# Activation table sets loaded by number, inverse roots from logarithm and exponential, and an expert layer read from a block-diagonal Gelu

## The chip, the cores and the metric

The kernel runs as one launch on one core of a Trainium2 chip. The metric is the device time of that core in microseconds. The core's engines are TensorE (PE in the profile, its weight loads PEld), VectorE (DVE), ScalarE (ACT), GpSimd (POOL) and SyncE (SP); each takes its instructions in order, and they wait for each other through semaphores.

## The reference

The input x is (8, 32, 16, 16): batch 8, 32 channels, 16 by 16 pixels. In float32, cut to what matters:

```python
x = x + conv_attention(_gn(x), ...)   # deformable attention, 4 heads, 16 sampled keys a head:
    # q, offset convolution, off / sqrt(var(off) + 1e-5), gelu, tanh, sigmoid,
    # grid_sample, softmax over 16 keys with a sampled position bias, output projection
t = _to_tokens(x)                     # (8, 256, 32)
t = t + self_attention(_ln_t(t))      # softmax(n @ n.T) @ n
t = t + experts(_ln_t(t), ...)
x = _from_tokens(t, x)

def _ln_t(v, eps=1e-05):
    m = jnp.mean(v, axis=-1, keepdims=True)
    s = jnp.var(v, axis=-1, keepdims=True)
    return (v - m) / jnp.sqrt(s + eps)

# experts: 16 experts, each picks the top 8 of the 256 tokens of a batch
probs = softmax(x @ gate_w.T + gate_b, axis=1)
topv, topi = top_k(probs, 8)                     # per batch and expert
pooled = sum_k topv * x[topi]                    # (8, 16, 32)
h = gelu(einsum('ebd,edh->ebh', [pooled, 1], weight1))   # 128 hidden
out = einsum('ebh,eho->ebo', [h, 1], weight2)            # 32 outputs
outputs[topi] += topv * out
```

Each of the 16 experts has its own `weight2` (128 by 32 and a bias row) and meets 8 rows, one per batch.

## The kernel before

There is no loop over tiles: everything stays in SBUF and PSUM, and the 128 partitions hold (batch, channels of a group), tokens, or (expert, batch) by turns. The order on each engine is written out by hand, with semaphores between the engines. The work runs in this order: group norm and q; convolution offsets with their norm, Gelu and tanh; sampled values and the position bias; attention logits, softmax (`d_max`, `d_sub`, `d_exp`, `d_sum`, `d_rec`, `d_prob`), transposes of the probabilities (L788), copies to `prob_t` (L584) and the attention output (L798); first layer norm (L591 to L596 on ACT, L1051 to L1056 on DVE); self-attention (L807 to L834, exponentials at L604); second layer norm (L619, L623 on ACT, L1076 to L1083 on DVE); gate (L883 to L901); experts (L915 to L933); two stores.

Both norms of tokens work alike, in two halves `h`: ACT squares into `ln_sq` or `u_sq`, DVE sums to `ln_ss`, ACT takes `Sqrt` into `ln_std`, DVE takes the reciprocal into `ln_rstd` and multiplies, giving `t1` or `t2`. PE turns both halves (L807, L876).

ACT needs the table set of a function loaded before it. `load_table(func)` (L503 to L508) runs a one-element activation of `func` on `warm`; the build puts an ACT_TABLE_LOAD ahead of it. It is called eight times: Sqrt, Gelu, Exp, Sqrt (after `d_exp`, L578), Exp (after the first norm's roots), Sqrt (after the copies `ot`, L615), Exp (after the second norm's roots), Gelu (after `g_exp`, L630).

The experts' second layer (L919 to L926) puts the 16 experts in four groups `q` of four. One matmul per group multiplies the 32 columns (expert, batch) of `hidden` with the 128 columns (expert, output) of `w2_sb`, and lands on 32 of the 128 partitions of `out2_ps`. So each row meets four experts' weights, and DVE keeps its own: it multiplies by the mask `row_slot` (L1116), sums over the four (L1117), and then scales for each batch (L1120).

`keep_busy(wait, bank)` (L649 to L652) issues `BUSY[wait]` matmuls of zeros on PE ahead of a wait; nobody reads them.

## Time and profile before

| | us |
|---|---|
| median of 3 runs | 65.18 (64.65, 65.18, 76.61) |
| the profiled execution's own time | 64.59 |
| its span, first to last instruction | 62.8 |

| engine | busy us | share of the span | instructions |
|---|---|---|---|
| PE | 53.7 | 86% | 579 |
| DVE | 38.4 | 61% | 96 |
| ACT | 34.3 | 55% | 70 |
| POOL | 21.0 | 34% | 44 |

The time outside the span is 64.59 - 62.8 = 1.8 us. The busy time of PE holds 16.1 us of zero matmuls (L652, 213 of them), so its share says little about what bounds the kernel. The chain of work that ended last is put down to PE for 46%, ACT 17%, DVE 16%, POOL 7%, and it passes from engine to engine every few tenths of a microsecond. The granted TensorE clock is 1.00 throughout.

### The profile page before, as it was taken

How to read it: one execution, taken by the hardware profiler on the slowest of the kernel's cores; microseconds unless marked ns; L12 is line 12 of the kernel's file. 1: busy time of each engine (PE TensorE's matmuls, PEld its weight loads, DVE VectorE, ACT ScalarE, POOL GpSimd, SP SyncE). 2: the span in 40 equal slices, each digit the busy share in tenths (PEclk: the TensorE clock that was granted, in tenths of full speed). 3: DMA queues.
4: the chain of work that ended last, by engine and by line, in shares of the span. 5: the costliest groups of instructions: out<-in, count | busy, mean ns of one | idle time of the engine just before them, and what ended most of it. 6: DMA issues, size and time to landing. Idle time of an engine off the chain costs nothing.

```text
span 62.8 us, 1442 instructions
## 1 busy us (share of the span) xinstructions
PE 53.7 (86%) x579; PEld 44.1 (70%) x579; DVE 38.4 (61%) x96; ACT 34.3 (55%) x70; POOL 21.0 (34%) x44
## 2 busy tenths in 40 slices
PE   3998997996996999999989939599997898989830
PEld 3997885954785899998979837334485586877700
DVE  3286698918499994599900652789969427540620
ACT  0901053969999041049957794988597628401020
POOL 3030489875779899000600000003000790000000
PEclk9999999999999999999999999999999999999999
DMA  0699921100000000000000000000000000000004
GB/s 0 202 188 229 276 70 47 57 8 0 0 0 0 0 10 0 0 0 0 0 0 0 16 5 0 0 0 0 0 0 0 0 10 0 0 0 0 0 18 149
DMA packets 3926, 2.02 MB, mean 32 GB/s; under 512 B 2640, under 2 KB 3792, under 8 KB 3920
## 3 DMA queue, kind: packets, MB, share of 16 engines
q1 hardware_dynamic: 1424, 1.37, 7.7%
q10 hardware_dynamic: 2496, 0.57, 4.2%
q8 instruction: 4, 0.07, 0.4%
q14 instruction: 2, 0.02, 0.1%
HBM read 1.67 MB, written 0.26 MB: 31 GB/s over the span
## 4 chain that ended last, share of the span: by engine, by line
PE 46%; ACT 17%; DVE 16%; POOL 7%; issue 5%; DMA 4%; DVEq 0%; ACTq 0%
PE ps L733 4%; DMA x_sb<-x_rows 4%; ACT L508 4%; ACT e_tok L604 4%; PE ps L829 3%; PE ps L777 3%; PE ps L726 3%; PE ps L798 3%; PE ps L755 3%; DVE taps L973 2%; POOL w_smp L468 2%; PE ps L813 2%; PE ps L652 2%; DVE off L975 2%; PE ps L933 2%
## 5 line engine op out<-in xcount | busy, mean ns | idle before, releaser
L652 PE MATMUL ps<-zeros 128*128 128x128 bf16 x213 | 16.1, 236 | 1.0 <-DVE zeros L950 1.0
L652 PEld LDWEIGHTS ps<-zeros 128*128 128x128 bf16 x213 | 14.7, 107 | 1.8 <-DVE zeros L950 1.0
L508 ACT ACT_TABLE_LOAD x8 | 10.3, 1283 | 1.8 <-PEq L1163 1.7
L604 ACT ACTIVATE e_tok<-ps,cst 128x1024 f32<-128x1024 f32 (+1 forms) x5 | 4.4, 941 | 1.1 <-PE ps L822 0.9
L381 POOL TENSOR_TENSOR c_scaled<-ln_c,e_sum 128x256 f32<-128x256 f32 x1 | 0.6, 622 | 11.7 <-DVE e_sum L1066 11.7
L1066 DVE TENSOR_REDUCE e_sum<-e_tok 128x4 f32<-128x1024 f32 x3 | 3.6, 1216 | 0.4 <-ACT e_tok L604 0.3
L1004 DVE COPY_PREDICATED ps<-over,ps 128x608 f32<-128x608 uint32 (+1 forms) x4 | 3.1, 778 | 0.8 <-PE ps L705 0.7
L829 PE MATMUL ps<-e_tok,t 128*32 128x256 f32 x32 | 3.1, 385 | 0.2 <-ACT e_tok L604 0.2
L705 PE MATMUL ps<-rpe_blk,minus_hat_rel 128*32 128x168 f32 x64 | 2.8, 316 | 0.5 <-DVE minus_hat_rel L1000 0.5
L491 POOL TENSOR_TENSOR o_n<-ln_c,e_rec 128x256 f32<-128x256 f32 x2 | 1.2, 621 | 5.9 <-DVE e_rec L1084 5.9
L568 ACT ACTIVATE kv<-ps,cst 128x256 f32<-128x256 f32 x4 | 1.7, 470 | 2.7 <-PE ps L726 2.7
L1051 DVE TENSOR_REDUCE ln_ss<-ln_sq 128x8 f32<-128x264 f32 x2 | 0.9, 428 | 3.7 <-ACT ln_sq L591 3.7
L421 POOL TENSOR_TENSOR wblk<-wts,cst 128x256 f32<-128x256 f32 x3 | 2.1, 684 | 2.9 <-DMA wts<-weights 2.9
L705 PEld LDWEIGHTS ps<-rpe_blk,minus_hat_rel 128*32 128x32 f32 x64 | 2.0, 142 | 1.3 <-issue 0.9
L813 PE MATMUL ps<-t_t 32*128 32x256 f32 x24 | 2.3, 400 | 0.8 <-ACT e_tok L604 0.8
L829 PEld LDWEIGHTS ps<-e_tok,t 128*32 128x32 f32 x32 | 1.2, 109 | 2.0 <-ACT e_tok L604 1.4
L376 POOL TENSOR_TENSOR d_prob<-d_exp,d_rec 128x512 f32<-128x512 f32 x1 | 1.1, 1057 | 4.5 <-DVE d_rec L1040 4.5
L574 ACT ACTIVATE d_exp<-d_sub 128x512 f32<-128x512 f32 x1 | 0.6, 629 | 3.4 <-DVE d_sub L1034 3.4
L1033 DVE TENSOR_REDUCE d_max<-ps 128x32 f32<-128x512 f32 x2 | 1.4, 691 | 1.7 <-PE ps L733 1.6
L524 ACT ACTIVATE xn_tok<-ps 128x512 f32<-128x512 f32 x1 | 0.6, 597 | 3.2 <-PE ps L669 3.2
L726 PE MATMUL ps<-xs,wblk 128*128 128x128 f32 x16 | 2.2, 281 | 0.1
L813 PEld LDWEIGHTS ps<-t_t 32*128 32x128 f32 x24 | 1.4, 184 | 1.2 <-ACT e_tok L604 1.2
(183 smaller groups left out, 127.3 us busy)
## 6 DMA issues: line engine op xcount, KB each, us to landing
w_sb<-weight ACTq DMA_DIRECT2D x1, 256.0 KB, 6.4
w_sb<-weight SPq DMA_DIRECT2D x1, 256.0 KB, 5.4
x_nat<-x_rows SPq DMA_DIRECT2D x8, 32.0 KB
wts<-weights SPq DMA_DIRECT2D x1, 192.5 KB, 4.6
cst<-shape_consts SPq DMA_DIRECT2D x1, 192.0 KB, 4.0
x_sb<-x_rows SPq DMA_DIRECT2D x1, 128.0 KB, 2.6
x_sb<-x_rows ACTq DMA_DIRECT2D x1, 128.0 KB, 2.8
cst<-shape_consts SPq DMA_DIRECT2D x1, 128.0 KB, 5.3
```

The source lines that it names most:

```text
L421: return nc.gpsimd.tensor_tensor(dst, src.unsqueeze(2).to_broadcast([P, n_groups, B, width]), same_b.unsqueeze(1).unsqueeze(3).to_broadcas ...
L508: nc.scalar.activation(warm[:, n:n + 1], zeros[:, 0:1], func)
L604: return nc.scalar.activation(dst, scores, ACT.Exp, bias=const("bound"))
L652: mm(bank(n_bank, P), zeros[:, :], zeros[:, :], start=True, stop=True)
L705: last = mm(row_ps[g][nx_rows(nx), 8 * yq:8 * yq + 8, 0:WIN], minus_hat_rel[:, yq, g * P + nx:(g + 1) * P:NK], rpe_blk[:, g].rearrange("p ...
L726: last = mm(kv_ps[w][:, g], wblk[:, 1 + w, gi, g].rearrange("p b o -> p (b o)"), xs[:, gi], start=(gi == 0), stop=(gi == G - 1))
L733: last = mm(lg_ps[:, h, g, :, hh], part[:, g, hh, 8 * h:8 * h + 8].rearrange("p y x -> p (y x)"), back_to_n[:, :].rearrange("p (t j) -> p ...
L755: mm(lg_ps[:, h, g].rearrange("p t k j -> p (t k j)"), q_sb[:, g, h * P:(h + 1) * P], kv[:, 0, g].rearrange("p t k j -> p (t k j)"), start ...
L813: last = mm(bank(s_banks[n][k])[:, M * h:M * h + M], t1_t[C * ((2 * n + k) % B4):C * ((2 * n + k) % B4) + C, n // 2, h * P:(h + 1) * P], t ...
L829: return mm(ot_ps[b // B4][rows], t1[:, h, b], e_tok[:, b, h], start=(h == 0), stop=(h == NHALF - 1))
L1004: return nc.vector.copy_predicated(row_ps[g][:, :, 0:width], mask.bitcast(U32).unsqueeze(2).to_broadcast([P, IMG * HG, width]), row_ps[g][ ...
L1066: reduce(e_sum[:, 2 * n:2 * n + 2], e_tok[:, 2 * n:2 * n + 2], AX.X, ALU.add).then_inc(e_sum_ready, 1)
```

## The change

- The four Sqrt and the four reciprocals of the two token norms become `Ln` and `Exp` with scale -0.5, both on ACT (`inverse_root`), with a wait of ACT for its own `Ln` between them. `ln_std` goes, `ln_log` comes.
- Gelu writes its 128 columns into the diagonal blocks of `hidden_blk` (four groups, four experts by four experts by eight batches), which GpSimd has zeroed at the start. The second layer is one matmul for each expert, 16 in all, with 32 stationary columns of which 8 are not zero, 32 moving ones, and accumulation over the four experts of a group. `out2_ps` has 32 columns, the bias matmul too. The mask and the sum on DVE go; the two scalings read `out2_ps` itself.
- `BUSY` has 0 in place of 12 zero matmuls before the transposes of the probabilities, and 6 in place of 15 before the last matmuls.

```diff
-    "d_prob_ready": 12, "prob_copied": 3, "t1_ready": 20, "t1_copied": 7, "t2_ready": 12,
-    "chosen_ready": 14, "pooled_ready": 4, "hidden_ready": 3, "out2_ready": 15,
+    "d_prob_ready": 0, "prob_copied": 3, "t1_ready": 20, "t1_copied": 7, "t2_ready": 12,
+    "chosen_ready": 14, "pooled_ready": 4, "hidden_ready": 3, "out2_ready": 6,
...
+SQRT_SET, LN_EXP_SET, GELU_SET = 3, 6, 10
...
-        hidden = sb("hidden", [P, NE, B])
-        own = sb("own", [P, E4, C])
-        out2 = sb("out2", [P, C])
+        hidden_blk = sb("hidden_blk", [P, EQ, E4, E4, B])
...
-        out2_ps = bank(7, E4 * C).rearrange("p (e o) -> p e o", e=E4)
+        out2_ps = bank(7, C)
...
+        def hidden_diagonal():
+
+            first = hidden_blk[:, :, 0, 0, :]
+            return bass.AP(tensor=first.tensor, offset=first.offset,
+                           ap=[list(first.ap[0]), [E4 * E4 * B, EQ], [E4 * B + B, E4], [1, B]])
...
+            nc.gpsimd.memset(hidden_blk[:, :, :, :, :], 0.0).then_inc(hidden_zeroed, 1)
...
-            warmed = [0]
-
-            def load_table(func):
-
-                n = warmed[0]
-                warmed[0] += 1
-                nc.scalar.activation(warm[:, n:n + 1], zeros[:, 0:1], func)
-
-            act.wait_ge(zeros_set, 1)
-            load_table(ACT.Sqrt)
+
+            def load_table(functions):
+
+                nc.scalar.add_instruction(mybir.InstLoadActFuncSet(
+                    name=nc.get_next_instruction_name(), act_func_set_id=functions, ins=[], outs=[]))
+
+            load_table(SQRT_SET)
...
-            load_table(ACT.Gelu)
+            load_table(GELU_SET)
...
-            load_table(ACT.Exp)
+            load_table(LN_EXP_SET)
...
-            load_table(ACT.Sqrt)
...
-            for h in range(NHALF):
-                act.wait_ge(ln_ss_ready, h + 1)
-                nc.scalar.activation(ln_std[:, 0, h], ln_ss[:, 0, h], ACT.Sqrt).then_inc(ln_std_ready, 1)
-            load_table(ACT.Exp)
+            def inverse_root(k, h):
+
+                act.wait_ge(ln_ss_ready, NHALF * k + h + 1)
+                nc.scalar.activation(ln_log[:, k, h], ln_ss[:, k, h], ACT.Ln).then_inc(ln_log_ready, 1)
+                act.wait_ge(ln_log_ready, NHALF * k + h + 1)
+                nc.scalar.activation(ln_rstd[:, k, h], ln_log[:, k, h], ACT.Exp, scale=-0.5).then_inc(ln_rstd_ready, 1)
+
+            for h in range(NHALF):
+                inverse_root(0, h)
...
-            load_table(ACT.Sqrt)
...
-                act.wait_ge(ln_ss_ready, NHALF + h + 1)
-                nc.scalar.activation(ln_std[:, 1, h], ln_ss[:, 1, h], ACT.Sqrt).then_inc(ln_std_ready, 1)
-            load_table(ACT.Exp)
+                inverse_root(1, h)
...
-            load_table(ACT.Gelu)
+            load_table(GELU_SET)
+            act.wait_ge(hidden_zeroed, 1)
             act.wait_ge(hidden_done, 1)
-            nc.scalar.activation(hidden[:, :, :], hid_ps.rearrange("p q e b -> p (q e) b"),
-                                 ACT.Gelu).then_inc(hidden_ready, 1)
+            nc.scalar.activation(hidden_diagonal(), hid_ps, ACT.Gelu).then_inc(hidden_ready, 1)
...
-            mm(out2_ps, ident, weight("bias2").unsqueeze(1).to_broadcast([P, E4, C]), start=True, stop=False,
-               skip_group_check=True)
+            mm(out2_ps, ident, weight("bias2"), start=True, stop=False, skip_group_check=True)
             pe.wait_ge(w2_loaded, 16)
             keep_busy("hidden_ready", 4)
             pe.wait_ge(hidden_ready, 1)
-            for q in range(EQ):
-                experts = slice(E4 * q, E4 * q + E4)
-                last = mm(out2_ps[E4 * B * q:E4 * B * q + E4 * B], hidden[:, experts].rearrange("p e b -> p (e b)"),
-                          w2_sb[:, experts], start=False, stop=True, skip_group_check=True)
+            for e in range(E4):
+                for q in range(EQ):
+                    last = mm(out2_ps[E4 * B * q:E4 * B * q + E4 * B],
+                              hidden_blk[:, q, e].rearrange("p f b -> p (f b)"), w2_sb[:, E4 * q + e],
+                              start=False, stop=(e == E4 - 1), skip_group_check=True)
...
-                dve.wait_ge(ln_std_ready, h + 1)
+                dve.wait_ge(ln_rstd_ready, h + 1)
                 dve.wait_ge(ln_c_ready, h + 1)
-                link(nc.vector.reciprocal(ln_rstd[:, 0, h], ln_std[:, 0, h]))
...
-                dve.wait_ge(ln_std_ready, NHALF + h + 1)
-                link(nc.vector.reciprocal(ln_rstd[:, 1, h], ln_std[:, 1, h]))
+                dve.wait_ge(ln_rstd_ready, NHALF + h + 1)
...
-            link(tt(own[:, :, :], out2_ps, const("row_slot").unsqueeze(2).to_broadcast([P, E4, C]), ALU.mult))
-            link(reduce(out2[:, :], own[:, :, :].rearrange("p e o -> p o e"), AX.X, ALU.add))
             for t in range(NT):
                 batches = slice(B4 * t, B4 * t + B4)
-                tt(out2_blk[:, batches], out2[:, :].unsqueeze(1).to_broadcast([P, B4, C]),
+                tt(out2_blk[:, batches], out2_ps.unsqueeze(1).to_broadcast([P, B4, C]),
```

**ScalarE, from the copies `ot` to the copy of the gate's logits** (second layer norm; `u_sq` are the squares, `t_t` the transposed tokens). Before:

```order
L615 ACTIVATE ot<-ps 128x256 [waits ot_done] x2
L508 ACT_TABLE_LOAD
L508 ACTIVATE warm<-zeros 128x1
L619 ACTIVATE u_sq<-ln_c 128x8x32 [waits ln_c_ready] x2
L623 ACTIVATE ln_std<-ln_ss 128x8 [waits ln_ss_ready] x2
L508 ACT_TABLE_LOAD
L508 ACTIVATE warm<-zeros 128x1
L626 ACTIVATE t_t<-ps 128x256 [waits t2_turned]
L628 ACTIVATE logits<-ps 128x256 [waits g_done]
```

Now:

```order
L621 ACTIVATE ot<-ps 128x256 [waits ot_done] x2
L624 ACTIVATE u_sq<-ln_c 128x8x32 [waits ln_c_ready] x2
L598 ACTIVATE ln_log<-ln_ss 128x8 [waits ln_ss_ready]
L600 ACTIVATE ln_rstd<-ln_log 128x8 [waits ln_log_ready]
L598 ACTIVATE ln_log<-ln_ss 128x8 [waits ln_ss_ready]
L600 ACTIVATE ln_rstd<-ln_log 128x8 [waits ln_log_ready]
L629 ACTIVATE t_t<-ps 128x256 [waits t2_turned]
L631 ACTIVATE logits<-ps 128x256 [waits g_done]
```

Two loads and their one-element activations are gone from this stretch, and the two square roots have become four short activations in a row.

**TensorE, from the projected values to the attention output** (`vo` in two products, then transposes of `d_prob`). Before:

```order
L777 MATMUL ps<-woblk_c,kv 128x128 [waits wkvo_ready,v_ready]
L777 MATMUL ps<-woblk_c,kv 128x128 x3
L777 MATMUL ps<-woblk,kv 128x128 x4
L652 MATMUL ps<-zeros 128x128 x12
L788 MATMUL ps<-cst,d_prob 128x128 [waits d_prob_ready0]
L788 MATMUL ps<-cst,d_prob 128x128 x3
L788 MATMUL ps<-cst,d_prob 128x128 [waits d_prob_ready1]
L788 MATMUL ps<-cst,d_prob 128x128 x3
L652 MATMUL ps<-zeros 128x128 x3
L798 MATMUL ps<-vo_c,prob_t 128x128 [waits prob_copied,vo_copied]
```

Now:

```order
L780 MATMUL ps<-woblk_c,kv 128x128 [waits wkvo_ready,v_ready]
L780 MATMUL ps<-woblk_c,kv 128x128 x3
L780 MATMUL ps<-woblk,kv 128x128 x4
L791 MATMUL ps<-cst,d_prob 128x128 [waits d_prob_ready0]
L791 MATMUL ps<-cst,d_prob 128x128 x3
L791 MATMUL ps<-cst,d_prob 128x128 [waits d_prob_ready1]
L791 MATMUL ps<-cst,d_prob 128x128 x3
L655 MATMUL ps<-zeros 128x128 x3
L801 MATMUL ps<-vo_c,prob_t 128x128 [waits prob_copied,vo_copied]
```

The transposes follow straight behind the projections; the 12 zero matmuls between them are gone.

**TensorE, from the experts' first layer to the last matmuls.** Before:

```order
L915 MATMUL ps<-pooled,w_sb 128x32 [waits pooled_ready]
L915 MATMUL ps<-pooled,w_sb 128x32 x3
L919 MATMUL ps<-wts,cst 128x128
L652 MATMUL ps<-zeros 128x128 [waits w2_loaded]
L652 MATMUL ps<-zeros 128x128 x2
L926 MATMUL ps<-w_sb,hidden 32x128 [waits hidden_ready]
L926 MATMUL ps<-w_sb,hidden 32x128 x3
L652 MATMUL ps<-zeros 128x128 x15
L933 MATMUL ps<-chosen,out_blk 128x256 [waits out2_ready] x2
```

Now:

```order
L918 MATMUL ps<-pooled,w_sb 128x32 [waits pooled_ready]
L918 MATMUL ps<-pooled,w_sb 128x32 x3
L922 MATMUL ps<-wts,cst 128x32
L655 MATMUL ps<-zeros 128x128 [waits w2_loaded]
L655 MATMUL ps<-zeros 128x128 x2
L928 MATMUL ps<-w_sb,hidden_blk 32x32 [waits hidden_ready]
L928 MATMUL ps<-w_sb,hidden_blk 32x32 x15
L655 MATMUL ps<-zeros 128x128 x6
L936 MATMUL ps<-chosen,out_blk 128x256 [waits out2_ready] x2
```

Four matmuls of 128 moving columns have become 16 of 32, the bias matmul has 32 columns, and 6 zero matmuls stand where 15 stood.

## Rows read from the trace of the kernel before

**Rows 1.** Instructions of line 508: durations in ns (min/median/max), first and last start, us.

```profile
L508 ACT ACT_TABLE_LOAD  x8: 1283/1283/1283, 1.7 to 52.6; - x8
L508 ACT ACTIVATE warm<-zeros x8: 202/203/203, 2.9 to 53.9; 128x1 f32<-128x1 bf16 x8
```

**Rows 2.** Timeline (start us, us, instruction, idle before and releaser), first Gelu.

```profile
11.02 1.73 PE L652 MATMUL ps<-zeros 128*128 128x128 bf16 x28
...
12.42 0.40 ACT L532 ACTIVATE off_blk<-off_nblk 128x256 f32<-128x256 f32 x1
```

**Rows 3.** Timeline, attention probabilities and their transposes.

```profile
29.73 1.06 POOL L376 TENSOR_TENSOR d_prob<-d_exp,d_rec 128x512 f32<-128x512 f32 x1 [4.47 <-DVE d_rec L1040]
...
30.65 0.69 DVE L376 TENSOR_TENSOR d_prob<-d_exp,d_rec 128x512 f32<-128x512 f32 x1
...
30.93 0.58 ACT L581 ACTIVATE vo_c<-ps 128x512 f32<-128x512 f32 x1
...
30.93 0.83 PE L652 MATMUL ps<-zeros 128*128 128x128 bf16 x12
...
31.60 1.04 PE L788 MATMUL ps<-cst,d_prob 128*128 128x128 f32 x8
...
32.24 1.09 ACT L584 ACTIVATE prob_t<-ps 128x512 f32<-128x512 f32 x2 [0.74 <-PE ps L788]
```

**Rows 4.** Timeline, roots of the first layer norm.

```profile
35.59 0.55 ACT L596 ACTIVATE ln_std<-ln_ss 128x8 f32<-128x8 f32 x2
...
36.41 0.19 DVE L1055 RECIPROCAL ln_rstd<-ln_std 128x8 f32<-128x8 f32 x1
...
36.64 0.42 DVE L1056 TENSOR_TENSOR t<-ln_c,ln_rstd 128x256 f32<-128x256 f32 x1
```

**Rows 5.** Timeline, roots of the second layer norm.

```profile
45.55 0.76 DVE L1076 TENSOR_TENSOR ln_c<-ps,c_scaled 128x256 f32<-128x256 f32 x2
...
46.44 0.71 ACT L619 ACTIVATE u_sq<-ln_c 128x256 f32<-128x256 f32 x2
...
46.87 0.76 DVE L1079 TENSOR_REDUCE ln_ss<-u_sq 128x8 f32<-128x264 f32 x2 [0.57 <-ACT u_sq L619]
...
47.33 0.54 ACT L623 ACTIVATE ln_std<-ln_ss 128x8 f32<-128x8 f32 x2 [0.19 <-DVE ln_ss L1079]
...
48.38 0.42 DVE L1083 TENSOR_TENSOR t<-ln_c,ln_rstd 128x256 f32<-128x256 f32 x1
```

**Rows 6.** Timeline, copy of the second norm's transpose and the gate.

```profile
49.30 0.36 ACT L626 ACTIVATE t_t<-ps 128x256 f32<-128x256 f32 x1
...
49.80 1.10 PE L883 MATMUL ps<-t_t,gate_blk 128*128 128x256 f32 x4
```

**Rows 7.** Timeline, second layer of the experts.

```profile
57.14 0.28 ACT L634 ACTIVATE hidden<-ps 128x128 f32<-128x128 f32 x1 [3.01 <-PE ps L915]
...
57.50 0.43 PE L926 MATMUL ps<-w_sb,hidden 128*32 128x128 f32 x8
...
58.00 0.29 DVE L1116 TENSOR_TENSOR own<-ps,cst 128x128 f32<-128x128 f32 x1 [2.03 <-PE ps L926]
...
58.73 0.49 DVE L1120 TENSOR_TENSOR out_blk<-out,row_rec 128x128 f32<-128x128 f32 x2
```

**Rows 8.** Timeline, other matmuls with 32 stationary columns.

```profile
13.93 0.42 PE L694 MATMUL ps<-wts,off_blk 128*32 128x1 f32 x16
...
53.82 1.19 PE L901 MATMUL ps<-picked_t,t 128*32 128x16 f32 x32
```

**Rows 9.** Line 901 (durations in ns, min/median/max; first and last start, us).

```profile
L901 PE MATMUL ps<-picked_t,t x32: 191/197/199, 53.8 to 54.8; 128*32 128x16 f32 x32
```

**Rows 10.** Timeline, GpSimd at the start.

```profile
0.84 0.23 POOL L417 MEMSET pooled<- 128x128 f32 x1
...
3.98 0.62 POOL L421 TENSOR_TENSOR wblk<-wts,cst 128x256 f32<-128x256 f32 x1 [2.91 <-DMA wts<-weights]
```

**Rows 11.** Stretches: busy us (count) PE, PEld, DVE, ACT, POOL; PEclk, DMA, GB/s.

```profile
57.00:62.80 5.80, 3.00 (x33) 2.06 (x32) 1.58 (x5) 0.66 (x2) 0.00 (x0) 1.00 0.13 45
```

More of the change, by code:

```diff
@@ L185, in build @@
         off_blk = sb("off_blk", [P, G, B, N])
-        warm = sb("warm", [P, 8])
         zeros = sb("zeros", [P, P], BF16)
@@ L237, in build @@
         ln_ss = sb("ln_ss", [P, 2, NHALF, B])
-        ln_std = sb("ln_std", [P, 2, NHALF, B])
+        ln_log = sb("ln_log", [P, 2, NHALF, B])
         ln_rstd = sb("ln_rstd", [P, 2, NHALF, B])
@@ L319, in build @@
         rpe_blk_ready, qpad_zeroed = sem("rpe_blk_ready"), sem("qpad_zeroed")
-        pooled_zeroed, zeros_set = sem("pooled_zeroed"), sem("zeros_set")
+        pooled_zeroed, hidden_zeroed, zeros_set = sem("pooled_zeroed"), sem("hidden_zeroed"), sem("zeros_set")
         q_done, q_copied = sem("q_done"), sem("q_copied")
@@ L343, in build @@
         prob_turned, prob_copied, att_done = sem("prob_turned"), sem("prob_copied"), sem("att_done")
-        ln_c_ready, ln_sq_ready, ln_ss_ready, ln_std_ready = (
-            sem("ln_c_ready"), sem("ln_sq_ready"), sem("ln_ss_ready"), sem("ln_std_ready"))
+        ln_c_ready, ln_sq_ready, ln_ss_ready, ln_log_ready, ln_rstd_ready = (
+            sem("ln_c_ready"), sem("ln_sq_ready"), sem("ln_ss_ready"), sem("ln_log_ready"), sem("ln_rstd_ready"))
         t1_ready, t1_turned = sem("t1_ready"), sem("t1_turned")
```

## The prediction

> **What bounds it now.** I read the chain of waits first, then the timeline around each edited line, then single lines for durations. No engine bounds the kernel. The chain goes from engine to engine, so an edit counts only by what it takes from that chain, and each one below is read where it stands. The eight table loads last 1.283 us each and the one-element activation behind each adds about 0.10 (0.20 long, with the next activation starting 0.11 after it) [rows 1]. That is 10.3 us of loads, four of which go. Most of it is no gain: a load costs only what it keeps the next activation from doing.
>
> **Start.** The set number spares the wait for the zeros and one short activation, at a time when ACT waits for data anyway: nothing.
>
> **First Gelu.** The load stays, the short activation goes. Gelu then starts at 12.31 instead of 12.42 and ends at 12.71. The zero matmuls on TensorE last until 12.75 [rows 2], so they are just no cover. Everything behind moves by 0.10 (between 0 and 0.11: nothing if the zero matmuls turn out the later ones). The load ahead of Exp has the same saving. It brings the copy `win` forward, but TensorE has no gap at the parts made from it, so I count nothing there.
>
> **Softmax to attention output.** The load behind `d_exp` ends ahead of the copy `vo_c` at 30.93, and this copy ends at 31.51, while `prob_t` starts at 32.24, released by the transposes of L788 [rows 3]. So that load was covered, and dropping it gains nothing by itself. The 12 zero matmuls were on the path: the first transpose starts 0.67 behind them (30.93 to 31.60) [rows 3]. What is late next is `d_prob`. GpSimd ends its half at 30.79. TensorE followed the end of another engine's result by 0.08 in the experts (57.42 to 57.50) [rows 7]; with 0.1 to 0.2 for GpSimd's the transposes start at 30.9 to 31.0, against 31.60. DVE ends the other half at 31.34 and four transposes take until about 31.4, so it does not hold them up. Gain 0.62, between 0.5 and 0.67.
>
> **Roots of the first norm.** A root of 8 columns lasts 0.21, by the 0.20 of one column [rows 1]; so ACT's first runs 35.59 to 35.80 and the second, which waits for its sum, 35.93 to 36.14 [rows 4]. Before, the first half then takes a reciprocal of 0.19 on DVE; now it takes an exponential of about 0.21 on ACT: no change, and `t1` of half 0 starts at about 36.07 still (0.34 ahead of the reciprocal behind it). For half 1 the reciprocal stood behind `t1` of half 0 on DVE until 36.41, and `t1` started at 36.64 [rows 4]. Now Ln of half 1 runs 35.93 to 36.14, Exp 36.17 to 36.38, and `t1` follows at 36.41. Gain 0.23. Ends: 0 (if ACT's wait for itself costs 0.1 each time) and 0.25. The load behind the roots goes too. The scores that come next wait for seven zero matmuls and for DVE's copy as well, so I take 0.03 for it, between 0 and 0.1.
>
> **Roots of the second norm.** Here a load was on the path. `u_sq` of half 0 started at 46.44, behind load and short activation, while its input, the first of two sums on DVE, was there at 45.97 (45.55 plus 0.42, the length of the like-sized `t2` row) [rows 5]. Now it starts at 45.99 and half 1, whose input ends at 46.31, at 46.33. Half 1 ends at 46.73 instead of 47.15. The sums `ln_ss` (0.42 each) end at 46.83 and 47.18 instead of 47.63. Ln and Exp: half 0 46.87 to 47.31, half 1 47.21 to 47.65. `t2` of half 1, which must also follow half 0 (47.33) by 0.34, starts at 47.67 instead of 48.38 [rows 5]. Gain 0.71, of which 0.45 is the load and the rest the reciprocals. Ends 0.5 and 0.75. What is late next: `ln_c` on DVE, which waits for the turned-back output.
>
> **Copy before the gate.** `t_t` started at 49.30, in the shadow of a load and its short activation, and the gate's matmuls started 0.14 behind the copy's end, at 49.80 [rows 6]. Only the last 0.11 of that shadow is sure to be the load's: DVE copies the other half at the same time, and TensorE's bias matmul stands ahead of the gate. Gain 0.08, ends 0 and 0.11.
>
> **Second layer.** The Gelu ends at 57.42 and L926 starts at 57.50, with the bias matmul and three zero ones done in time [rows 7]; a shorter bias matmul gains nothing. The four old matmuls (eight passes in the trace) take until 57.97, and the scaling starts at 58.73: 0.76 for mask and sum, which go [rows 7]. Against it stand 16 matmuls, 32 passes, in place of eight. The trace has two bounds for the distance between such passes. At L694 eight matmuls of 32 stationary columns go round the four groups of output partitions, as the new ones will: 16 passes in 0.42. At L901 sixteen stay in one group: 32 passes in 1.19 [rows 8]. One pass of the latter lasts 0.197 by itself [rows 9]. So the passes start (0.42 - 0.20)/15 = 15 ns apart in the one and (1.19 - 0.20)/31 = 32 ns in the other; the old L926, with 128 moving columns over four groups, gives about (0.43 - 0.28)/7 = 21. The new ones rotate like L694, and I take 17 ns: 31 x 0.017 + 0.23 = 0.76, done at 58.26. The scaling starts at 58.28 instead of 58.73, and is no slower from PSUM (the mask took 0.29 from there, the scaling 0.29). Gain 0.45. With 32 ns it is 1.22 and no gain (-0.03); with 15, 0.51. Six zero matmuls at 0.06 (12 took 0.67) [rows 3] end before the first scaling, so cutting them from 15 only keeps them out of the way. The Trainium skill ("TensorE: Matmul & The Clock Gate", section "Wait — 56ns, not 53.3ns?") says that start-to-start never drops below about 25 ns however few columns there are. By it this term would be 31 x 0.025 + 0.23 = 1.0 and the gain 0.2. L694 contradicts it with 15 ns, at one moving column.
>
> **Zeroing.** GpSimd's `pooled` of 128 columns took 0.23, so 512 take at most 0.92; they fit in the 2.91 us that GpSimd waits for the weights [rows 10]. Nothing.
>
> **Sum.** 0.10 + 0.62 + 0.23 + 0.03 + 0.71 + 0.08 + 0.45 = 2.22. Against the profiled execution's own 64.59 this gives 62.4; nothing outside the span changes. That execution agrees with the lowest of the three runs (64.65) and is 0.9% below their median (65.18), so the figure may come out some tenths higher. With all low ends the sum is 1.0 (63.6), with all high ones 2.4 (62.2).
>
> **Rivals.**
> - *The small matmuls are paced by themselves.* For: nothing in the trace has 32 of them in rotation with 32 moving columns, and L901 shows 32 ns. Against: L694. At 32 ns the sum is 1.74 and the time 62.9. If each matmul took 62 ns a pass, 1.92 + 0.23 = 2.15 would make this part 0.94 slower than before, the sum 0.83 and the time 63.8; both L694 and L901 speak against it. The same page of the Trainium skill, same section, has such a figure (about 62 ns a matmul where its sequencer decodes it). Chance 0.15 for the 32 ns, 0.04 for 63.8.
> - *The roots don't overlap.* ACT waits for its own Ln four times, and what is queued behind is the other half. If each wait costs 0.1 to 0.15 more, the norms give 0.5 instead of 0.94: 62.9 at full pace elsewhere, 63.3 together with a slow second layer. For: no row shows a chain of dependent short activations. Chance 0.10.
> - *The loads come back (slower).* If something places a load ahead of each Ln and each Exp as separate functions, eight loads of 1.28 stand in the two chains of roots. All but about 0.5 us of them is on the path, which gives 62.4 + 9.8 = 72. It decides from the second load on a chain: 2 x 1.28 is more than the whole gain. Against it: the program as built holds four loads and no other, and before it held the eight that the trace shows. The Trainium skill ("ScalarE: Activation LUTs", "Table sets: the hidden batching unit") says that a pass of the compiler's back end puts a load before every activation that needs one, and also that one set has both functions. Chance 0.03.
> - *TensorE's clock falls (slower).* 21 zero matmuls go. Before, the granted clock is 1.00, and it is so even in the last stretch, where TensorE is busy for 3.0 of 5.8 us [rows 11]. The gaps in which they stood get shorter, too. At 1.2 GHz from the transposes to the scores, about 3.5 us of TensorE on the path would double: 66. Chance 0.02.
>
> **Numbers.** Chance of the forecast as summed, 62.4 with 61.9 to 62.8 around it: 0.66. Range 61.9 to 63.6: it takes in the slow second layer, the slow roots and most low ends together, and the few tenths between the runs before. This kernel can be told from no change at about 2%, 1.3 us. The sum is below this only with nearly all low ends together, or with matmuls at 62 ns, or where the runs differ: same 0.11. Slower 0.05, from the last two rivals. Faster 0.84.
>
> **What would show it.** Four loads in ACT's row. L791 starting right behind L780, and `prob_t` about 0.7 earlier than before. `u_sq` starting behind `ln_c`, not behind ACT. Each Exp of a root 0.02 to 0.04 behind its Ln. 32 passes of L928 in 0.75 and the scaling 0.03 behind. Wrong would be: passes over 30 ns apart, `t2` held by the zero matmuls ahead of the transposes, a clock below 1.00, or a fifth load.

## The result and the profile after

| | before | after |
|---|---|---|
| median, us | 64.92 (4 runs, 64.62 to 76.61) | 62.70 (4 runs, 62.67 to 62.78) |
| ratio to before, without the 76.61 | | 0.969, 95% interval 0.965 to 0.973 |
| profiled execution, us | 64.59 | 62.78 |
| its span, us | 62.8 | 60.7 |
| what lies outside the span, us | 1.8 | 2.1 |
| zero matmuls | 213 | 192 |

One run of the kernel before took 76.61 us and stays out of the ratio; the other three took 64.62, 64.65 and 65.18. The kernel is 3.1% faster, 62.7 us against a forecast of 62.4 and a range of 61.9 to 63.6. The granted clock stayed at 1.00 in the profile. Below, the lines of after that answer to the rows of before; times are us from the span's start.

The shares by engine of the chain that ended last (part 4 of the page), and the table loads (part 5):

```profile
PE 57%; DVE 11%; ACT 10%; POOL 7%; issue 5%; DMA 4%; DVEq 0%; ACTq 0%
...
L510 ACT ACT_TABLE_LOAD x4 | 5.1, 1283 | 1.7 <-PEq L1162 1.7
```

PE's share rose from 46% to 57% and ACT's fell from 17% to 10%: loads and roots have left the chain. The rise of PE is in part a matter of ties. Zero matmuls hold 6% of this chain (L655, 3.4 us) where they held 2% (L652, 1.2 us), because at three places they now end within 0.1 us of the result that TensorE waits for, as at the first Gelu below, and the chain is then led through them.

The timeline around the first Gelu (start, us, instruction, idle before and releaser; columns as in [rows 2]):

```profile
11.12 1.28 ACT L510 ACT_TABLE_LOAD   x1
...
11.12 1.73 PE L655 MATMUL ps<-zeros 128*128 128x128 bf16 x28
...
12.41 0.42 ACT L534 ACTIVATE off_blk<-off_nblk 128x256 f32<-128x256 f32 x1
...
12.88 1.13 PE L691 MATMUL ps<-off_blk,wts 128*128 128x256 f32 x4
```

The Gelu starts 0.01 behind the end of the load, and the zero matmuls end at 12.85, against the Gelu's 12.83. The two end 0.02 apart, so the zeros hold up the next matmuls by no more than that, as forecast [rows 2].

The timeline from the projected values to the attention output:

```profile
29.74 1.06 POOL L380 TENSOR_TENSOR d_prob<-d_exp,d_rec 128x512 f32<-128x512 f32 x1 [4.53 <-DVE d_rec L1043]
...
30.24 0.60 ACT L582 ACTIVATE vo_c<-ps 128x512 f32<-128x512 f32 x1 [0.73 <-PE ps L780]
...
30.93 1.12 PE L791 MATMUL ps<-cst,d_prob 128*128 128x128 f32 x8
...
31.57 1.12 ACT L585 ACTIVATE prob_t<-ps 128x512 f32<-128x512 f32 x2 [0.73 <-PE ps L791]
```

`vo_c` starts 0.69 earlier than before and nobody gains from it. The transposes start at 30.93, and `prob_t` at 31.57 instead of 32.24 [rows 3].

The timeline of the first norm's roots, and from the view of one line the waits that stand in DVE's queue as instructions of their own (durations in ns, first and last start):

```profile
34.92 0.21 ACT L598 ACTIVATE ln_log<-ln_ss 128x8 f32<-128x8 f32 x1
...
35.16 0.21 ACT L600 ACTIVATE ln_rstd<-ln_log 128x8 f32<-128x8 f32 x1
...
35.28 0.19 ACT L598 ACTIVATE ln_log<-ln_ss 128x8 f32<-128x8 f32 x1
...
35.40 0.92 DVE L1058 TENSOR_TENSOR t<-ln_c,ln_rstd 128x256 f32<-128x256 f32 x2 [0.18 <-ACT ln_rstd L600]
...
35.50 0.21 ACT L600 ACTIVATE ln_rstd<-ln_log 128x8 f32<-128x8 f32 x1
...
36.38 0.66 PE L810 MATMUL ps<-cst,t 128*128 128x128 f32 x4 [0.92 <-DVE t L1058]
```

```profile
L1057 DVEq EVENT_SEMAPHORE  x2: 21/21/21, 34.8 to 35.4; - x2
```

Logarithm and exponential take turns between the halves as forecast: the second exponential ends at 35.71. But the two multiplications take 0.92 together, at 0.43 each (0.77 in the second norm, below), so the second starts 0.49 behind the first and ends at 36.32. It has two waits, and one of them is an instruction by itself.

The timeline of the second norm's roots and of the gate:

```profile
44.81 0.76 DVE L1078 TENSOR_TENSOR ln_c<-ps,c_scaled 128x256 f32<-128x256 f32 x2
...
45.26 0.75 ACT L624 ACTIVATE u_sq<-ln_c 128x256 f32<-128x256 f32 x2 [0.99 <-DVE ln_c L1078]
...
45.71 0.76 DVE L1081 TENSOR_REDUCE ln_ss<-u_sq 128x8 f32<-128x264 f32 x2 [0.15 <-ACT u_sq L624]
...
46.18 0.21 ACT L598 ACTIVATE ln_log<-ln_ss 128x8 f32<-128x8 f32 x1 [0.17 <-DVE ln_ss L1081]
...
46.66 0.77 DVE L1084 TENSOR_TENSOR t<-ln_c,ln_rstd 128x256 f32<-128x256 f32 x2 [0.18 <-ACT ln_rstd L600]
...
47.14 0.78 PE L879 MATMUL ps<-cst,t 128*128 128x128 f32 x4
...
47.84 0.38 ACT L629 ACTIVATE t_t<-ps 128x256 f32<-128x256 f32 x1 [0.88 <-PE ps L879]
...
48.37 1.10 PE L886 MATMUL ps<-t_t,gate_blk 128*128 128x256 f32 x4
```

`u_sq` starts 0.45 behind the start of `ln_c` where it was 0.89 [rows 5]: no longer behind ACT's own load.

The timeline of the experts' second layer, and the durations of its passes in ns (min/median/max):

```profile
55.76 0.28 ACT L638 ACTIVATE hidden_blk<-ps 128x128 f32<-128x128 f32 x1 [3.28 <-PE ps L918]
...
56.09 0.46 PE L928 MATMUL ps<-w_sb,hidden_blk 128*32 128x32 f32 x32
...
56.63 0.49 DVE L1119 TENSOR_TENSOR out_blk<-ps,row_rec 128x128 f32<-128x128 f32 x2 [2.10 <-PE ps L928]
...
56.98 1.13 PE L936 MATMUL ps<-chosen,out_blk 128*128 128x256 f32 x4
```

```profile
L928 PE MATMUL ps<-w_sb,hidden_blk x32: 196/196/217, 56.1 to 56.4; 128*32 128x32 f32 x32
```

The 32 passes take 0.46, hardly more than the eight old ones (0.43) [rows 7]. That is on average (0.46 - 0.20)/31 = 8.5 ns from start to start.

**The ledger.** Each line is the time from one landmark to the next, from the starts in both profiles.

| from, to | before | after | gain | forecast |
|---|---|---|---|---|
| span's start to the first statistics of x | 3.36 | 3.46 | -0.10 | 0 |
| to the matmuls behind the first Gelu | 9.51 | 9.42 | 0.09 | 0.10 |
| to the first `prob_t` | 19.37 | 18.69 | 0.68 | 0.62 |
| to the transposes of `t1` | 4.88 | 4.81 | 0.07 | 0.23 |
| to the first exponential of the scores | 1.74 | 1.74 | 0.00 | 0.03 |
| to DVE's copy of the transposed `t2` | 10.48 | 9.83 | 0.65 | 0.71 |
| to the gate's matmuls | 0.46 | 0.42 | 0.04 | 0.08 |
| to the experts' Gelu | 7.34 | 7.39 | -0.05 | 0 |
| to the scaling | 1.59 | 0.87 | 0.72 | 0.45 |
| to ACT's last copy | 1.52 | 1.51 | 0.01 | 0 |
| outside the span | 1.79 | 2.08 | -0.29 | 0 |

Behind the first statistics of x, and inside the span, the gains add up to 2.21 (2.22 forecast).

### The profile page after: what moved, and what is told of

It is laid out like the page before. It is cut to its first block, busy times and chain, and to the rows that moved or that the text cites. A ratio compares the mean times of both kernels' runs of the same rounds, so it can differ in the third digit from the quotient of the medians.

```text
span 60.7 us, 1436 instructions
## 1 busy us (share of the span) xinstructions
PE 52.4 (86%) x582; PEld 43.0 (71%) x582; DVE 37.0 (61%) x90; ACT 28.8 (48%) x62; POOL 21.5 (35%) x45
## 4 chain that ended last, share of the span: by engine, by line
PE 57%; DVE 11%; ACT 10%; POOL 7%; issue 5%; DMA 4%; DVEq 0%; ACTq 0%
PE ps L655 6%; DMA x_sb<-x_rows 4%; PE ps L736 4%; ACT e_tok L610 4%; PE ps L832 3%; PE ps L729 3%; PE ps L780 3%; PE ps L801 3%; PE ps L758 3%; PE ps L871 3%; DVE taps L976 2%; POOL w_smp L473 2%; PE ps L816 2%; DVE off L978 2%; PE ps L691 2%
## 5 line engine op out<-in xcount | busy, mean ns | idle before, releaser
L655 PE MATMUL ps<-zeros 128*128 128x128 bf16 x192 | 14.7, 237 | 1.0 <-DVE zeros L953 1.0
L655 PEld LDWEIGHTS ps<-zeros 128*128 128x128 bf16 x192 | 13.4, 108 | 1.6 <-DVE zeros L953 1.0
L665 PE MATMUL ps<-xn,wblk 128*128 128x256 f32 x8 | 2.0, 388 | 0.3 <-DVE xn L969 0.3
```

Source lines behind the costliest of these rows:

```text
L655: mm(bank(n_bank, P), zeros[:, :], zeros[:, :], start=True, stop=True)
L665: last = mm(q_ps[g], wblk[:, 0, gi, g].rearrange("p b o -> p (b o)"), xn[:, gi].rearrange("p (y x) -> p y x", y=IMG), start=(gi == 0), sto ...
```

## The experiments

All times are set beside runs of the kernel before on the same chip; these had medians of 64.78, 64.71 and 64.70 us in the three groups. The changed kernel, run again in the third group, had 62.78. Where no edit stands, the stretches of the ledger repeat to 0.01 or 0.02 us from kernel to kernel, medians to 0.1 or 0.2. Two stretches do not. The first statistics of x come between 3.21 and 3.55 us. The stretch behind them, to the matmuls behind the first Gelu, takes 9.41 or 9.42 in seven profiles of the change and its versions, but 9.53 to 9.97 in five others, and 9.97 in the changed kernel itself when it ran again. In that profile DVE's first products of the projections (L976) start at 7.56 instead of 6.96, at a granted clock of 1.00; why is not shown. So every version below is read from the landmarks behind this place.

### Where the 0.68 us ahead of the attention output came from

```diff
-    "d_prob_ready": 0, "prob_copied": 3, "t1_ready": 20, "t1_copied": 7, "t2_ready": 12,
+    "d_prob_ready": 12, "prob_copied": 3, "t1_ready": 20, "t1_copied": 7, "t2_ready": 12,
```

> The changed kernel with its 12 zero matmuls ahead of the probabilities' transposes put back. Theory (they stood on the path, and the table load behind the exponentials was covered): the transposes start about 0.67 us later and everything behind them moves by as much, 62.7 + 0.67 = 63.4 us. Rival (the load that went from this place gave the gain, the zeros filled a wait for the probabilities): the transposes wait until then anyway, no change, 62.7 us.

Measured: 63.33 us (ratio 0.9765, 0.974 to 0.979), 0.6 slower than the change. Its timeline at the transposes:

```profile
30.01 0.60 ACT L582 ACTIVATE vo_c<-ps 128x512 f32<-128x512 f32 x1 [0.73 <-PE ps L780]
...
30.70 0.83 PE L655 MATMUL ps<-zeros 128*128 128x128 bf16 x12
...
31.37 1.04 PE L791 MATMUL ps<-cst,d_prob 128*128 128x128 f32 x8
...
32.02 1.09 ACT L585 ACTIVATE prob_t<-ps 128x512 f32<-128x512 f32 x2 [1.41 <-PE ps L791]
```

From the matmuls behind the Gelu to `prob_t` it takes 19.39, as before (19.37). The zeros stood on the path.

The counterpart takes them out of the kernel before and leaves its loads:

```diff
-    "d_prob_ready": 12, "prob_copied": 3, "t1_ready": 20, "t1_copied": 7, "t2_ready": 12,
+    "d_prob_ready": 0, "prob_copied": 3, "t1_ready": 20, "t1_copied": 7, "t2_ready": 12,
```

> The kernel before with only these 12 zero matmuls taken out, all its eight table loads kept. Theory: the copy of the projected values still starts behind the load at 30.93 and ends at 31.5 us, just ahead of the first transposed probabilities, so the full 0.67 us comes without dropping a load: about 0.67 below the kernel before. Rival: the load behind the exponentials now holds the copies back and keeps part of it, 0.3 us or less.

Measured: 63.94 us (0.9865, 0.984 to 0.989), 0.84 faster.

```profile
29.69 1.28 ACT L508 ACT_TABLE_LOAD   x1
...
31.09 0.58 ACT L581 ACTIVATE vo_c<-ps 128x512 f32<-128x512 f32 x1
...
31.10 1.12 PE L788 MATMUL ps<-cst,d_prob 128*128 128x128 f32 x8
...
31.73 1.12 ACT L584 ACTIVATE prob_t<-ps 128x512 f32<-128x512 f32 x2
```

The load is still there, `vo_c` ends at 31.67, and `prob_t` starts at 31.73. The same stretch takes 18.71, as in the change (18.69). So about 0.66 us, a third of the whole gain, needs nothing but a 0 in a table, and dropping the load here was worth nothing. The median moved by 0.17 more than the stretch; I put no meaning into that.

### The table loads

Four loads again, behind `d_exp`, the roots of the first norm, the copies `ot` and the roots of the second norm:

```diff
             nc.scalar.activation(d_exp[:, 1], d_sub[:, 1], ACT.Exp).then_inc(d_exp_ready, 1)
+            load_table(LN_EXP_SET)
...
             for h in range(NHALF):
                 inverse_root(0, h)
+            load_table(LN_EXP_SET)
...
                 nc.scalar.activation(ot[:, t], ot_ps[t], ACT.Copy).then_inc(ot_copied, 1)
+            load_table(LN_EXP_SET)
...
             for h in range(NHALF):
                 inverse_root(1, h)
+            load_table(LN_EXP_SET)
```

> The changed kernel with a table load of 1.28 us put back at each of the four places where one went (the same set again, without the one-element activation). Theory (a load costs what it keeps the next activation from): behind the exponentials 0; behind the first norm's roots it ends at 37.0, so the copy of the transposed tokens starts 0.16 late, 0.1 to 0.15 on the path; behind the copies of the attention output the squares start 0.33 late; behind the second norm's roots the copy ahead of the gate starts 0.4 late: together about 0.9 us, 63.6 us. Rival (the loads were nearly all hidden and the reciprocals gave the gain): 0.45 us or less. Second rival (each load on the chain costs its whole length): 3 x 1.28 = 3.8 us.

Measured: 63.71 us (0.9855, 0.982 to 0.990), 0.9 to 1.0 slower.

```profile
36.96 0.38 ACT L608 ACTIVATE t_t<-ps 128x256 f32<-128x256 f32 x1
...
44.41 1.28 ACT L510 ACT_TABLE_LOAD   x1
...
45.70 0.72 ACT L627 ACTIVATE u_sq<-ln_c 128x256 f32<-128x256 f32 x2
...
47.42 1.28 ACT L510 ACT_TABLE_LOAD   x1
...
48.72 0.38 ACT L633 ACTIVATE t_t<-ps 128x256 f32<-128x256 f32 x1
```

By landmarks: 0.02 ahead of `prob_t`, 0.17 from the transposes of `t1` to the scores, 0.33 to the copy of `t2`, 0.43 to the gate. Together 0.95, and each load costs what it keeps from starting, between nothing and 0.43 of its 1.28. The load behind the second norm is the surprise of the ledger. In the kernel before, this load and its short activation cost the ledger 0.04; with the roots done earlier on the same engine the load alone would cost 0.43. So more than half of the 0.65 gained ahead of this place is kept only because this load went too.

### Reciprocals and roots

```diff
-                nc.scalar.activation(ln_log[:, k, h], ln_ss[:, k, h], ACT.Ln).then_inc(ln_log_ready, 1)
-                act.wait_ge(ln_log_ready, NHALF * k + h + 1)
-                nc.scalar.activation(ln_rstd[:, k, h], ln_log[:, k, h], ACT.Exp, scale=-0.5).then_inc(ln_rstd_ready, 1)
+                nc.scalar.activation(ln_log[:, k, h], ln_ss[:, k, h], ACT.Abs).then_inc(ln_log_ready, 1)
...
+                link(nc.vector.reciprocal(ln_rstd[:, 0, h], ln_log[:, 0, h]))
```

> The changed kernel with its four table loads, but in both token norms one activation on ACT (an absolute value, which leaves out the root and the logarithm) and the reciprocal on DVE, as long as before. Theory (the exponential on ACT lets the two halves overlap where the reciprocal on DVE doesn't): the first norm is 0.07 us slower, since there the second half gained only that, the second norm about 0.2 slower: 0.25 to 0.3 us, 63.0 us. Rival (both norms give the 0.23 and 0.26 that the prediction put down): 0.5 us, 63.2 us. Second rival: four activations where two would do cost something, and this is faster.

By landmarks the first norm takes 4.87 instead of 4.81 (0.06 slower), the stretch with the second 10.07 instead of 9.83 (0.24 slower): the 0.3 of the theory. The median is 63.59 us (0.982, 0.977 to 0.986), 0.8 to 0.9 slower than the change; a further 0.34 lies between the gate and the experts' Gelu (7.73 instead of 7.39), all of it directly ahead of the Gelu, where its data differ and no edit stands, and 0.1 at the start. I can't explain that part, and read this kernel by its two norms alone.

```profile
35.52 0.42 DVE L1057 TENSOR_TENSOR t<-ln_c,ln_rstd 128x256 f32<-128x256 f32 x1
...
35.87 0.19 DVE L1056 RECIPROCAL ln_rstd<-ln_log 128x8 f32<-128x8 f32 x1
...
36.09 0.42 DVE L1057 TENSOR_TENSOR t<-ln_c,ln_rstd 128x256 f32<-128x256 f32 x1
```

Here too the reciprocal of half 1 stands behind half 0's multiplication, as in [rows 4].

### The second wait

```diff
+            dve.wait_ge(ln_c_ready, NHALF)
             for h in range(NHALF):
                 dve.wait_ge(ln_rstd_ready, h + 1)
-                dve.wait_ge(ln_c_ready, h + 1)
...
-            load_table(GELU_SET)
             act.wait_ge(hidden_zeroed, 1)
+            load_table(GELU_SET)
```

> The changed kernel with DVE's wait for the centred values of the first norm taken ahead of the loop (once, for both halves), so that the second multiplication has only one wait, and ACT's wait for the zeroed blocks taken ahead of the last table load, so that the Gelu has only one. Theory (a second wait ahead of an instruction keeps it from overlapping its predecessor): the second multiplication of the first norm starts 0.34 behind the first instead of 0.50, which gives 0.16 us, and the Gelu starts about 0.05 earlier: 62.5 us. Rival (the second multiplication was late for its exponential, not for its waits): no change, 62.7 us.

```profile
35.79 0.76 DVE L1058 TENSOR_TENSOR t<-ln_c,ln_rstd 128x256 f32<-128x256 f32 x2 [0.25 <-ACT ln_rstd L600]
```

The two multiplications take 0.76 instead of 0.92, so the second wait was what kept them apart: the second now starts 0.34 behind the first, before its end, instead of 0.07 behind its end. The first starts 0.10 behind its exponential instead of 0.03, so part of it is lost again; the norm takes 4.72 instead of 4.81, and the stretch to the experts' Gelu 7.34 instead of 7.39. The forecast of 62.5 us was missed: the median is 62.93 (0.972, 0.968 to 0.976). It says little at this size, since in the profile the stretch to the matmuls behind the first Gelu was 0.37 longer. It ran again beside the changed kernel:

> The changed kernel once more, on the same chip and in the same rounds as the three below, since runs of different days and chips differ by some tenths: 62.7 to 62.9 us, and a start of the chain (the landing of x) that moves by up to 0.3 us from profile to profile.

> The kernel with the two waits taken ahead, again, now beside the changed kernel on one chip. In its first profile the second multiplication came 0.34 behind the first instead of 0.50, but the first came 0.08 later behind its exponential, and the Gelu 0.05 earlier. Theory: 0.1 to 0.15 us less than the changed kernel. Rival (the first multiplication's delay eats it): no difference.

Measured: 62.78 us for the change (0.971, 0.968 to 0.974), 62.66 for the version with single waits (0.9685, 0.965 to 0.972). The landmarks repeat (4.72 instead of 4.80, 7.33 instead of 7.39: 0.14 together); the medians differ by 0.12, and the intervals overlap. This version is the fastest that ran, and not told apart from the change by time.

### The second layer

```diff
-            for e in range(E4):
-                for q in range(EQ):
-                    last = mm(out2_ps[E4 * B * q:E4 * B * q + E4 * B],
-                              hidden_blk[:, q, e].rearrange("p f b -> p (f b)"), w2_sb[:, E4 * q + e],
-                              start=False, stop=(e == E4 - 1), skip_group_check=True)
+            for q in range(EQ):
+                experts = slice(E4 * q, E4 * q + E4)
+                last = mm(out2_ps[E4 * B * q:E4 * B * q + E4 * B], hidden[:, experts].rearrange("p e b -> p (e b)"),
+                          w2_sb[:, experts], start=False, stop=True, skip_group_check=True)
...
+            link(tt(own[:, :, :], out2_ps, const("row_slot").unsqueeze(2).to_broadcast([P, E4, C]), ALU.mult))
+            link(reduce(out2[:, :], own[:, :, :].rearrange("p e o -> p o e"), AX.X, ALU.add))
```

> The changed kernel with the second expert layer as before: four matmuls, mask and sum on DVE, 15 zero matmuls. Theory (the small matmuls cost 0.46 us, about as much as the four old ones, so the whole of mask and sum was gained): 0.69 us slower, 63.4 us, all of it between the Gelu and the scaling. Rival (as the prediction had it, 17 ns from pass to pass): 0.45 us slower, 63.15 us.

Measured: 63.04 us (0.973, 0.970 to 0.976), 0.3 slower; from Gelu to scaling 1.59 instead of 0.87, 0.72 slower.

```profile
55.98 0.42 PE L924 MATMUL ps<-w_sb,hidden 128*32 128x128 f32 x8
...
56.48 0.29 DVE L1112 TENSOR_TENSOR own<-ps,cst 128x128 f32<-128x128 f32 x1 [2.03 <-PE ps L924]
...
57.21 0.49 DVE L1116 TENSOR_TENSOR out_blk<-out,row_rec 128x128 f32<-128x128 f32 x2
```

The two figures don't agree, and the difference is not in the span. Its four runs leave 1.76 to 1.83 us outside the span, like all 25 of the kernel before in these groups (1.75 to 1.88) and the four of the kernel before without zeros (1.77 to 1.85). All runs of the change and of its variants with the new layer leave 1.97 to 2.16. So the new layer gives 0.72 in the span, loses 0.05 to the Gelu's second wait and about 0.24 outside. That leaves 0.4, against the 0.3 between the medians; the theory's 63.4 did not come. What of the layer costs the 0.24 (the zeroing of 512 columns, the buffer, the number of matmuls) is open: no run took these apart.

```diff
-            for e in range(E4):
-                for q in range(EQ):
+            for q in range(EQ):
+                for e in range(E4):
```

> The changed kernel with the two loops around the 16 small matmuls exchanged, so that the four experts of one group of output partitions follow each other; work and zeros unchanged. Theory (they are 8.5 ns apart because neighbours go to different groups): passes fall to about 32 ns apart as at the pooling matmuls, 1.19 us instead of 0.46, and the kernel is 0.7 us slower, 63.4 us. Rival (the pace doesn't depend on the order): 0.46 us and 62.7 us.

Measured: 63.20 us (0.9745, 0.971 to 0.978), 0.4 to 0.5 slower.

```profile
56.27 0.90 PE L928 MATMUL ps<-w_sb,hidden_blk 128*32 128x32 f32 x32
...
57.20 0.49 DVE L1119 TENSOR_TENSOR out_blk<-ps,row_rec 128x128 f32<-128x128 f32 x2 [2.50 <-PE ps L928]
```

The same 32 passes take 0.90: on average (0.90 - 0.20)/31 = 23 ns apart instead of 8.5. The order of the two loops is worth 0.4 us.

Neither average is the distance of any two neighbours. The starts of the single passes in the two traces, in ns from the first:

| passes | starts |
|---|---|
| change, passes 1 to 16 | 0 7 14 20, 53 60 66 73, 85 91 98 105, 116 123 130 136 |
| loops exchanged, first eight of one group | 0 53 84 116 148 179 211 243 |
| loops exchanged, next eight | 153 206 238 269 301 333 364 396 |

In the second version the starts mix, and I sort them into four rows of eight; the first of each row lasts 217 ns and the others 196, which supports this. Read so, a group of output partitions takes its second pass 53 ns behind its first and then one every 32 ns, in both kernels, as L901 does in its one group. In the change four groups do this side by side, 7 ns apart. With the loops exchanged a group begins only 153 ns behind the one before it, and overlaps its last three passes. So the theory's 32 ns was right within a group, and its 1.19 us was too much because neighbouring groups overlap.

### The zero matmuls and the clock

```diff
-    "d_prob_ready": 0, "prob_copied": 3, "t1_ready": 20, "t1_copied": 7, "t2_ready": 12,
-    "chosen_ready": 14, "pooled_ready": 4, "hidden_ready": 3, "out2_ready": 6,
+    "d_prob_ready": 0, "prob_copied": 0, "t1_ready": 0, "t1_copied": 0, "t2_ready": 0,
+    "chosen_ready": 0, "pooled_ready": 0, "hidden_ready": 0, "out2_ready": 0,
```

> The changed kernel without any zero matmul from the attention on (62 more go; those ahead of the projections stay). Theory (the gaps that they fill are under 1.2 us each, and real matmuls come between): the granted clock stays at 1.00 and the kernel is the same or up to 0.1 us faster. Rival (the zeros hold the clock): the clock falls to 1.2 GHz somewhere behind 32 us, matmuls there take about twice as long, and the kernel is 2 to 6 us slower.

The zeros left out are 69 (3 + 20 + 7 + 12 and 14 + 4 + 3 + 6), not the 62 of the expectation.

Measured: 65.64 us, from 63.79 to 66.56, mean clocks of 0.96 to 0.875. The theory fell. The profile caught the mildest run; the clock by slices of 1.5 us, and from its timeline the first matmuls behind the attention output:

```profile
PEclk9999999999999999999999999999999999998555
...
36.40 0.66 PE L810 MATMUL ps<-cst,t 128*128 128x128 f32 x4 [2.04 <-DVE t L1058]
```

Then each half of the zeros by itself:

> The changed kernel without the 42 zero matmuls between the probabilities' transposes and the second norm; the later 27 stay. With all 69 out the granted clock fell at about 57 us in the profile, with means of 0.875 to 0.96 in the runs. Theory (the clock falls for what TensorE did shortly before, so only the late zeros hold it): clock 1.00 to the end and 62.7 us. Rival (the early gaps count as well): the clock falls in some run, before 57 us, and the kernel is over 0.5 us slower.

> The changed kernel without the 27 zero matmuls from the gate on; the 42 earlier ones stay. Theory (the late gaps, 1.1 us ahead of the chosen tokens' transposes and several of 0.3 to 0.5 in the experts, let the clock fall at the end): as with all of them out, clock means below 0.97 in some runs and 63.5 to 66 us. Rival (it took both): clock 1.00 and 62.7 us.

Without the early ones: 64.38 us, single runs of 62.62, 64.35, 64.41 and 65.53 with clocks of 0.995, 0.942, 0.941 and 0.919. Without the late ones: 64.03 us (0.9885, 0.985 to 0.992), clocks of 0.93 to 0.956 in all four. Stretches of both profiles (busy us and count of PE, PEld, DVE, ACT, POOL; granted clock; DMA), the first two of the early variant, the next two of the late one, and the late one's last matmuls:

```profile
34.00:36.00 2.00, 0.32 (x3) 0.13 (x2) 1.36 (x4) 1.39 (x7) 0.00 (x0) 1.00 0.00 0
...
38.00:46.00 8.00, 7.60 (x62) 4.25 (x62) 4.88 (x5) 4.77 (x6) 0.62 (x1) 0.50 0.01 2
```

```profile
50.00:52.00 2.00, 0.93 (x6) 0.56 (x5) 1.53 (x7) 1.33 (x3) 0.42 (x1) 1.00 0.00 0
...
56.00:58.00 2.00, 1.42 (x35) 1.09 (x36) 0.49 (x2) 0.18 (x1) 0.00 (x0) 0.50 0.00 0
```

```profile
57.38 2.08 PE L936 MATMUL ps<-chosen,out_blk 128*128 128x256 f32 x4 [0.40 <-DVE out_blk L1119]
```

In the early variant TensorE is idle from 34.3 to 36.35, in the roots of the first norm; the clock is at 1.2 GHz from 36.4, with TensorE busy for 7.60 of the 8 us up to 46, and back at 2.4 at 46.7. In the late one the clock falls at 55.8. Ahead of that TensorE is busy for less than half of the stretch in which the gate chooses tokens, and idle for another 0.5 ahead of the experts' first layer; which of the two counts is not shown. The last matmuls then take 2.08 instead of 1.13. The same idle stretch of 2.0 us did not always bring the clock down: one run of the early variant (62.62) escaped, and so did the profile without any zeros, at 1.00 until 56.8. So what decides is not the program alone. The theory for the early half fell and that for the late half held: both count.

## Why the prediction was right, and where it was not

The sum is better than its terms. Inside the span 2.21 came for 2.22, but the second layer gave 0.27 more than forecast, the softmax 0.06 more, and the other terms together about as much less. That they cancel is luck. (The high ends of the terms add up to 2.5, not the 2.4 of the prediction; nothing hangs on it.)

- **First Gelu**: 0.09 for 0.10, and the load ahead of Exp nothing, as put. Only the timelines show it: no run took this activation by itself.
- **Softmax to attention output**: 0.68 for 0.62. The load was covered and the zeros were not, shown from both sides by two runs. The size was off because the 0.62 lets the transposes start 0.19 behind the end of GpSimd's `d_prob` (30.79 to 30.98); they started 0.13 behind it (30.80 to 30.93).
- **Roots of the first norm**: 0.07 for 0.23, the mis-sized term. The chain on ACT ran to the hundredth as worked out: the exponential of half 1 ends 0.79 behind the start of the first logarithm (34.92 to 35.71; 35.59 to 36.38 forecast). I let the second multiplication follow this exponential at once and did not see that it has two waits; it came 0.49 behind the first multiplication, and 0.19 behind the exponential. With one wait it came 0.34 behind the first, and the first came 0.07 later, so that 0.09 of the missing 0.16 came back. The 0.03 for the load behind these roots did not show in the ledger (0.00), yet the load put back costs 0.17.
- **Roots of the second norm**: 0.65 for 0.71, and the steps came in the order in which they were put. What is missing went in small delays on ACT and DVE: `t2` of half 1 starts 2.20 behind the start of `ln_c` (47.01 and 44.81), where 2.12 was forecast and 2.83 stood before. The 12 zeros ahead of its transposes end level with `t2` of half 0 and hold nothing up. The experiments split the gain as the prediction did: 0.33 for the load ahead of the squares (0.45 forecast together with its short activation, which no run took by itself) and 0.24 for the roots (0.26 forecast).
- **Copy before the gate**: 0.04 for 0.08, within its bounds. The four loads put back show that this place mattered more than its term: 0.43.
- **Second layer**: 0.72 for 0.45. I took 17 ns between passes from L694's average; they came 8.5 ns apart. What I averaged away is the pace of one group. L694 gives the same group its next pass after 60 ns (starts at 0, 82, 143, 203 ns), L901 after 32, and L928 behaved like L901: four groups side by side at 32 ns each make 8 ns from pass to pass. So both the 15 ns and the 32 ns of [rows 8] were read right and combined wrongly. Why L694 is slower is not shown; its weight loads last 156 ns, those of L928 113. The floor of 25 ns in the Trainium skill ("TensorE: Matmul & The Clock Gate", section "Wait — 56ns, not 53.3ns?") agrees with the 32 ns within one group and does not hold between groups, where starts are 7 ns apart. Two small slips lie in the same term: the old matmuls ended at 57.93, not 57.97, and DVE starts 0.07 to 0.08 behind the last of them, not 0.02.
- **Zeroing**: "Nothing" was right for GpSimd's queue, which waits for the weights anyway. But the Gelu's wait for it cost 0.05 (with the wait ahead of the load it is gone), and the step "nothing outside the span changes" failed: about 0.24 went there, for a cause that is open. The profiled execution took 62.78, 0.4 more than forecast: 0.29 outside the span and 0.10 at the start, which moves by as much between profiles of one kernel.
- **Rivals**: slow matmuls and non-overlapping roots did not come. There were four loads and no fifth. The clock held, but for another reason than I gave. I argued that the gaps got shorter; what the runs show is that the zeros still left hold it, and that without the early half it falls in three of four runs and without the late half in all four.

## What to carry to other kernels

Price an instruction by what it keeps from starting and not by its length: four table loads of 1.28 us put back cost 0.95 together, nothing at one place and 0.43 at another, and moving the neighbours changes that price. Small matmuls that accumulate into several groups of output partitions should go round the groups in the inner loop (0.4 us for 16 of them here). An average distance between passes is a poor price for others: look at the starts, and at which passes share a group. Filler matmuls must be tried one wait at a time: 12 of them cost 0.66 to 0.70 us, and 69 others are worth 1 to 4 us, run by run, by keeping the clock.

## What the hardware showed that was not expected

- Matmul passes with 32 stationary and 32 moving columns start, as I read the single starts, 32 ns apart within one group of output partitions; passes of different groups start 7 ns apart and run side by side. Over 32 passes this makes 8.5 ns from pass to pass in rotation, and 23 group by group.
- An instruction with two waits of its own has one of them as a separate instruction in the queue (21 ns): a multiplication on DVE with two waits came 0.49 us behind its predecessor, with one 0.34.
- Without the early zeros the profile has the clock at 1.2 GHz from 36.4 to 46.7 us, behind 2.0 us in which TensorE stood idle, and one run of four had hardly any of it. Without any zeros the profile has the same idle stretch and no fall behind it. Without the late ones the fall stands at 55.8, behind the stretch of the gate's choice (50 to 52), and not in it. So the same program can lose 0 or 3 us by it.
- The time outside the span was 1.75 to 1.88 us in every run of the experiments that had the old second layer and 1.97 to 2.16 with the new one, with the same transfers. The cause is open.
